# The output product of an attention sequence moves one slot later, behind the next scores

## The reference, cut to what matters

```python
q = (query @ Wq + bq); k = (key @ Wk + bk); v = (value @ Wv + bv)
...
attn = jax.nn.softmax(scores, axis=-1)
ctx = jnp.einsum('bhts,bshd->bthd', attn, v).reshape(B, T, H * Dv)
out = ctx @ Wo + bo
...
x = _layernorm(x + _L0_xattn_ref(x, ctx_1024, ctx_1024, ...), axis=-1)
```

## Time and profile before

| | |
|---|---|
| median of 3 runs | 1636.52 us (1636.0 to 1638.09) |
| the profiled execution, its own time | 1619.51 us |
| its span, first to last instruction | 1617.8 us |
| TensorE busy | 1348.5 us, 83% |
| VectorE busy | 956.1 us, 59% |
| ScalarE busy | 946.5 us, 59% |
| GpSimd busy | 834.8 us, 52% |
| granted TensorE clock, mean | 0.938 |

### The profile page before, as it was taken

The page is one execution under the profiler, slowest core; times in us unless marked ns, Lnnn a source line. Parts: engine busy times, 40 slices in busy tenths (PEclk is TensorE's granted clock), DMA queues, the critical chain, the costliest instruction groups (busy, mean ns, idle before and its releaser), DMA issues. The chain is left out here.

```text
span 1617.8 us, 34460 instructions
## 1 busy us (share of the span) xinstructions
PE 1348.5 (83%) x11280; PEld 1098.5 (68%) x11280; DVE 956.1 (59%) x2616; ACT 946.5 (59%) x3395; POOL 834.8 (52%) x988
## 2 busy tenths in 40 slices
PE   2889897999898988899898998989988998967542
PEld 1667676777786777678776777767776777756442
DVE  3456565565655666566764777556665776555324
ACT  3666656576756666466755667565665766555111
POOL 4343525543555457554556546654566646547244
PEclk9999998999998999889998999989999999989777
DMA  6000000032212312222212212132122212135563
GB/s 207 8 7 8 7 7 15 26 93 59 60 38 83 96 30 67 63 79 78 64 43 69 81 55 71 42 99 79 37 60 82 82 57 61 37 94 154 157 181 84
DMA packets 149425, 109.99 MB, mean 68 GB/s; under 512 B 12736, under 2 KB 144384, under 8 KB 149248
## 3 DMA queue, kind: packets, MB, share of 16 engines
q1 hardware_dynamic: 139328, 89.43, 19.0%
q0 software_dynamic: 8192, 16.79, 3.6%
q10 hardware_dynamic: 1728, 1.57, 0.3%
HBM read 73.14 MB, written 34.60 MB: 67 GB/s over the span
## 5 line engine op out<-in xcount | busy, mean ns | idle before, releaser
L1791 POOL TENSOR_TENSOR pr<-pr,ri 128x480 f32<-128x480 f32 x256 | 251.1, 995 | 303.4 <-DVE ri L1394 299.9
L1068 ACT ACTIVATE pr<-sE,nm 128x120 f32<-128x120 f32 x512 | 178.1, 360 | 240.3 <-DVE nm L1389 222.3
L1056 ACT ACTIVATE pT<-t 120x512 f32<-120x512 f32 x256 | 142.3, 614 | 78.7 <-PE t L528 72.8
L1068 ACT ACTIVATE pr<-sO,nm 128x120 f32<-128x120 f32 x512 | 179.2, 381 | 0.0
L669 PEld LDWEIGHTS sE<-kT,qT 64*128 64x128 f32 x1024 | 131.1, 197 | 55.3 <-issue 55.3
L711 PE MATMUL pvb<-wo,hT 128*128 128x128 f32 x1024 | 137.4, 290 | 31.7 <-DVE hT L1404 31.7
L669 PE MATMUL sO<-kT,qT 64*128 64x120 f32 x1024 | 156.7, 295 | 7.0 <-issue 7.0
L1404 DVE TENSOR_TENSOR hT<-pvb,col 128x512 f32<-128x512 f32 x128 | 87.9, 686 | 126.0 <-PE pvb L702 111.4
L711 PEld LDWEIGHTS pvb<-wo,hT 128*128 128x128 f32 x1024 | 125.8, 200 | 45.5 <-DVE hT L1404 45.0
L669 PE MATMUL sE<-kT,qT 64*128 64x120 f32 x1024 | 155.7, 295 | 0.5 <-issue 0.5
L1820 POOL DMA_INDIRECT sorted_x<-x,slot x128 | 129.8, 1014 | 47.3 <-issue 34.3
(11 more groups left out here) (382 smaller groups left out, 3525.7 us busy)
## 6 DMA issues: line engine op xcount, KB each, us to landing
wq<-in_w_e SPq DMA_DIRECT2D x232, 128.0 KB
sorted_y<-yq SPq DMA_DIRECT2D x68, 256.0 KB
xq<-sorted_x SPq DMA_DIRECT2D x58, 256.0 KB
xt<-in_x SPq DMA_DIRECT2D x16, 256.0 KB, 2.9
sorted_x<-yq SPq DMA_DIRECT2D x16, 256.0 KB, 4.2
cT<-in_ctxT SPq DMA_DIRECT2D x16, 240.0 KB, 3.0
out_y<-y SPq DMA_DIRECT2D x48, 64.0 KB
sorted_x<-x,slot POOLq DMA_INDIRECT x128
```

Source lines behind the costliest of these rows:

```text
L1056: f(pT[:, 4 * r:4 * r + 4, :], seqs((t0, t1)[r][0:S, :]), ACT.Copy).then_inc(sem[f"probsT{r}_sb"], 1)
L1068: ins = f(pr[:, p % RING, r, i, :], score_banks[r][:, i * S:(i + 1) * S], ACT.Exp, bias=nm[:, p % 2, r, i:i + 1], accum_out=rsum[:, p % 2, ...
L1791: GP.tensor_tensor(pr[:, p % RING, r, :, :], pr[:, p % RING, r, :, :], ri[:, p % 2, r, :, :].to_broadcast([P, 4, S]), ALU.mult).then_inc(s ...
```

## The change

`b_wo(q)`, `b_sum(q)` and `b_ln2(q)` and their GpSimd part `ln(q)` for q = 0, 1, 2 move one slot later. TensorE issues the product in the even slot, right behind that slot's transposes and scores. VectorE takes the sum in that slot behind the maxima, and `b_ln2` in the odd slot after it, also behind the maxima. GpSimd takes `ln` in the even slot. For q = 3 the product, sum and `ln` stay at the end of slot 9. The number of instructions is unchanged.

```diff
@@ TensorE @@
                     if B and 0 < s < PAIRS:
                         b_scores(b, s)
+                    if B and s > LAG + 1 and not odd:
+                        b_wo(b, (s - LAG) // 2 - 1)
...
-                    if B and s > LAG and odd:
-                        b_wo(b, (s - LAG) // 2)
+                    if B and s == PAIRS + LAG - 1:
+                        b_wo(b, SEQ - 1)
@@ VectorE @@
                         b_max(b, s)
                     if B and s > LAG + 1 and not odd:
+                        b_sum(b, (s - LAG) // 2 - 1)
+                    if B and s > LAG + 1 and odd:
                         b_ln2(b, (s - LAG) // 2 - 1)
...
-                    if B and s > LAG and odd:
-                        b_sum(b, (s - LAG) // 2)
+                    if B and s == PAIRS + LAG - 1:
+                        b_sum(b, SEQ - 1)
@@ GpSimd @@
-                    if B and s > LAG and odd:
-                        ln(b, (s - LAG) // 2, 2, mv2[:], ve2[:], rs2[:])
+                    if B and s > LAG + 1 and (not odd or s == PAIRS + LAG - 1):
+                        ln(b, (s - LAG) // 2 - (not odd), 2, mv2[:], ve2[:], rs2[:])
```

## The result

| | before | after |
|---|---|---|
| median | 1636.26 us (6 runs, 1627.1 to 1638.09) | 1592.97 us (6 runs, 1588.6 to 1595.14) |
| the profiled execution, its own time | 1619.51 us | 1589.15 us |
| its span | 1617.8 us | 1587.4 us |
| granted TensorE clock, mean | 0.938 | 0.938 |

The ratio is 0.9752 (95% interval 0.9728 to 0.9776): 2.5% faster, some 40 us by the ratio and 43 us between the two medians. The prediction was 22 us, with a range that ended at 1599: the sign was right and the size was not. Brackets behind a ratio are always its 95% interval. The two traces stand only 30.4 us apart, because the first traced execution was short for the kernel before.

The account below looks back on a forecast made before the run. The prediction took TensorE's queue as the chain, its length changing only through waits on it. Terms 0 + 4 + 8 + 10 = 22 us, taken off the median 1636.5, gave 1614.5 us, 1.3% faster; range 1599 to 1637.

Parts of the forecast that it names:

- Slots 3 and 4, 0 us: Product q = 0: same matmuls in either order, and b_pv(2)'s wait for the later sum hidden by 0.3 us; gain 0.
- Slots 5 and 6, 4 us: Product q = 1: b_ln2 leaves VectorE's stretch before hs, 0.25 to 0.85 us per body, 3.8 to 12.8 in all; 4 taken.
- GpSimd term, put at 0: ln(q) shifts the gathers and context split by 0.8 us, users two slots later: cost 0, at most a few tenths per body.
- clock, put at 0: The sum had no term for TensorE's half-clock stretches; changes in them appeared only in the rivals.
- The other worry of that paragraph: b_ln2 in slot 5 could stretch by 1 to 2 us behind a gather, through the port pair VectorE and GpSimd share.
- Slots 7 and 8, 8 + 10 us: Product q = 2 and b_ln2(2): 8 us less wait for hT, 10 us less wait for the copy kT.
- kT, predicted 10: Slot 8: with b_ln2(2) in slot 9, the copy kT no longer queues behind 1/std; all 10.1 us of TensorE's wait go.
- hT, predicted 8: Slots 7 and 8: transposes run first and cover 10.0 us of the wait for hT; late xn takes about 2; term 8.
- (1): VectorE's chain in slots 5 and 6 follows earlier exponentials and some half-clock stretches go: 34 us gain, 1602 us; chance 0.15.
- (2): Half clock at new places, behind slot 6's waits in eight more bodies: 14 us lost, 8 left, 1628 us; chance 0.15.
- (3): The next wait (xn, hs or the experts' transfers) takes the gain back: 0 to 3 us left, 1635 us; chance 0.12.
- (4): The sum behind the maxima is paid: b_pv waits 1.5 us in slots 4 and 6, 22 us slower, 1658 us; chance 0.10.

Follow-up runs that it names:

- only_q0: Kernel before with product, sum, ln and b_ln2 of q = 0 alone one slot later (kind A): 1552.08 us, ratio 0.9974.
- sum_first_slot6: Whole change, but in slot 6 VectorE takes the sum of q = 1 ahead of the maxima (kind B): 1598.75 us, ratio 0.9781.
- all_three: The whole change, written with a parameter, against the kernel before on a chip of kind A: 1515.35 us, ratio 0.9746.
- wo01_ln2_slot9: Kernel before with q = 0 and 1 moved as in the whole change, of q = 2 only b_ln2, to slot 9 (kind B): 1610.71 us, ratio 0.985.
- before_3: The kernel before, unchanged, traced again on a chip of kind B: 1629.47 us, ratio 0.9986.
- all_three_2: The whole change once more, beside the kernel before on one chip of kind B: 1595.91 us, ratio 0.9775.
- wo2_ln2_stays: Kernel before with product, sum and GpSimd part of q = 2 one slot later, b_ln2(2) left in slot 8 (kind A): 1593.58 us, ratio 1.0236.
- only_q1: Kernel before with product, sum, ln and b_ln2 of q = 1 alone one slot later (kind A): 1547.12 us, ratio 0.9941.
- floor_and_sum6: Whole change, slot 7's a_floored ahead of the last sum, and one-group bodies' slot 5 last sum in slot 6 behind hs: 1579.96 us, again 1577.08.

## Why the prediction was wrong

The steps that failed, in short. The forecast of 1614.5 us was 21.5 us too high. Some 8 us of this are in the sum: the traces stand 30.4 us apart where it had 22. Behind slot 7 it is 27.4 us against 18, because waits there were priced too low and the clock was put at 0; everything else together is 3.0 against 4. The other 13 us are in the basis: the traced execution that the 22 us were taken from stood 16.7 us below its median, that of after 3.8 below its own. 30.4 us off the median of before would have been 1606 us, inside the range.

**What bounds the kernel: right.** TensorE's queue was the chain, and the time went where a wait on it went.

**Slots 3 and 4, 0 us: right.** The order alone gave 0.03 us in each odd body of only_q0, `b_pv(2)` waits for nothing but 0.5 us in bodies 0 to 2.

**Slots 5 and 6, 4 us: the mechanism right, the sum wrong.** The new wait lies inside that for hs (sum_first_slot6), and hs comes 0.25 us earlier. But the wait for hs was measured from gin, and what stands ahead of gin on VectorE was taken to be unchanged. On kind B it isn't. TensorE, VectorE and GpSimd in slot 5 of body 8, after (kind B) and then all_three (kind A):

```profile
784.27 1.09 PE L702 MATMUL pvb<-pT,vv 120*64 120x128 f32 x16
...
787.82 0.69 DVE L1406 TENSOR_TENSOR hT<-pvb,col 128x512 f32<-128x512 f32 x1 [3.54 <-remote]
...
784.85 0.97 POOL L1841 DMA_INDIRECT gat<-sorted_y,slot  x1 [0.30 <-issue]
786.12 1.01 POOL L1824 DMA_INDIRECT sorted_x<-x,slot  x1 [0.30 <-issue]
```

```profile
769.31 1.09 PE L702 MATMUL pvb<-pT,vv 120*64 120x128 f32 x16
...
770.45 0.69 DVE L1406 TENSOR_TENSOR hT<-pvb,col 128x512 f32<-128x512 f32 x1 [1.13 <-PE pvb L702]
...
769.89 0.97 POOL L1841 DMA_INDIRECT gat<-sorted_y,slot  x1 [0.30 <-issue]
771.16 1.01 POOL L1824 DMA_INDIRECT sorted_x<-x,slot  x1 [0.30 <-issue]
```

hT starts 3.55 us behind the first matmul of `b_pv(3)` in one and 1.14 in the other, with GpSimd doing the same. In the kernel before it was 2.46 in this place (`b_pv(3)` at 802.43, hT at 804.89), where the last indirect DMA ended 1.8 us behind the start of `b_pv(3)`; in after it ends at 787.13, 2.9 us behind. So hT comes later by as much as the norm `ln` shifts the gathers, 1 us. In even bodies 6 to 14 the stretch from slot 5 to 7 went from 15.7 to 16.8 us up to 16.9 to 17.8, and on kind A down from 14.9 to 16.9 to 14.5. Two steps failed here. One is the **GpSimd term, put at 0**: the prediction saw the shift of 0.8 us, and looked only at who uses the gathers; wo01_ln2_slot9 shows the same in slot 7. The other, and larger one, is the **clock, put at 0** in the sum. In these five even bodies the stretch grew by 6.5 us in the first pair and by 10.0 in the later one; 6.0 and 6.7 of this are the cost of half clock, and only 0.2 and 2.6 more idle time of TensorE. That is the second rival, in these slots: `b_pv(4)` waits 2.6 to 2.9 us for xa in them and a half-clock stretch follows. On kind A, where hT isn't late, both idle time and half clock fall. That the late hT brings the half clock about fits this, but no run tests it alone. What links a gather and hT of another engine is shown as timing here; its mechanism is open. The other worry of that paragraph, a `b_ln2` stretched by 1 to 2 us, didn't come: the longest of the 64 in after took 0.86 us, 0.53 before.

**Slots 7 and 8, 8 + 10 us: the steps of the sum that failed most.** The mechanism was right; measured were 27.4 us in the two first traces. Term by term, from start to start:
- kT, predicted 10: 11.9 us in the first trace and in before_3 (brackets 10.1), 15.8 on kind A. The step that failed is that a wait was priced by its bracket; each cost 0.16 us more.
- hT, predicted 8: from 19.0 to 9.0 us, so 10.0; in before_3 and all_three_2 from 18.8 to 8.4. The 10 us of the cover were right; the 2 us taken off for a late xn didn't come on this kind (0.4 us of waits for xn in after within the bodies). On kind A they did, and were 5.
- The clock, predicted 0 and, in the first rival, at most 3 for the whole kernel: half clock behind slot 7 costs 6.9 us before and 2.7 in after, 4.2 less; 4.6 less from before_3 to all_three_2; 9.0 less on kind A. wo2_ln2_stays shows the same with its sign turned, 20.7 us more. The prediction had no term for the clock behind the waits that it took away.
- These make 11.9 + 10.0 + 4.2 = 26.1 of the 27.4.

The Trainium skill (TensorE: Matmul & The Clock Gate, What's actually happening) has the clock follow how busy TensorE has been of late. The runs agree in the main: kernels with less waiting in slots 7 and 8 show less half clock there, and the one with more waiting shows more. But the link is loose. only_q1 lost 7.8 us of half-clock cost there while TensorE's idle time fell by 1.1, and two traces of one kernel, floor_and_sum6, differ by 3.4 us there. So that the clock gave these us is shown; that the removed waits alone made it do so is not. Nor does half clock fall everywhere: over the whole trace it goes from 201.5 to 197.8 us in the first pair, from 213.9 to 219.0 in the pair on kind B later, and from 144.7 to 127.7 on kind A.

**The basis: the step that put the number outside the range.** The prediction applied differences of the trace to the median. The first traced execution was 17 us below it and before_3 shows that such an execution isn't typical; the waits of both are alike in slots 7 and 8 (10.1 us for kT in both), so this moved no term. In the other runs the traced execution stood from 7.8 us below to 8.9 above its median. By the medians the gain is 43, 40 and 36 us, in the traces 30, 33 and 30. Executions of the kernel before on kind B range over 24 us (1616 to 1641), and their body 15 differs by 9.6 us from trace to trace. Where the last 5 to 10 us of the medians lie is open.

**The rivals.** (1) the chain of slots 5 and 6 follows: refuted for kind B, while on kind A those slots gave 9.2 us. By its number, 1602 us, it came nearest, and that was luck: most of the gain was in another place. (2) more half clock in slot 6: on kind B it is there, 10.3 us of cost from slot 5 to 7 in after against 6.7, but outweighed behind slot 7. (3) and (4): refuted, (4) by sum_first_slot6.

## What to carry to other kernels

Price a wait on TensorE from start to start, against a place where the same pair of matmuls stands without one: here that was 0.16 us more than the bracket for each wait, on some of 0.2 us nearly as much again. Look also at what half clock costs in the matmuls behind it, and don't count on all of it: from trace to trace of one kernel it moved by up to 5 us in a stretch. One traced execution isn't the median; take a second before its time is used as a basis. If an instruction must wait for a slow engine's result, look at what is queued behind it: one step of 0.34 us, moved by a slot, gave 22 us, and left where it was it turned the same edit into a loss of 37. And before a shift on an engine that nobody seems to wait for is put at nothing, look at what the other engines do in those microseconds.

## What the runs showed of the hardware

The chips of these runs fall in two kinds for this kernel, 1555 and 1632 to 1636 us, 5% apart; the whole change gives 2.5% and 2.2 to 2.5% on them. One difference is the clock: 144.7 us at half clock in the trace of kind A, 201.5 and 213.9 in those of kind B. Another is the one above. On kind B hT starts, with VectorE idle, more than 0.9 us behind the start of its last matmul 11 to 13 times in the kernel before and 20 or 21 times in the whole change. Each time an indirect DMA of GpSimd is being issued as `b_pv` ends, and mostly hT follows the end of one by 0.5 to 0.8 us. On kind A this happens not once, though 13 or 14 times a DMA is being issued then too, and on kind B 3 to 8 such cases stay on time; otherwise an idle VectorE starts hT 0.32 to 0.37 us behind the matmul's start, on both kinds. Why is open. I had read the late hT of even bodies as VectorE's queue.
